# One decoder layer on one core: weight quantising cut into five pieces on GpSimd, down weights turned one stage earlier, the last tile in halves, the first batch in pairs with two gates made ahead

## What is computed

```
x = x + L0_attn(layernorm(x))          # products, running sums over tokens, products
x = x + L0_xattn(layernorm(x), ctx)    # causal softmax attention over the batch and 77 context rows, and a gate
x = x + L0_ffn(layernorm(x))
def fp4_quant_dequant(x):              # blocks of 16 along the last dim
    scale = max(max|x| / 6, 1e-12)     # then each value goes to the nearest of 0, .5, 1, 1.5, 2, 3, 4, 6 times scale
L0_ffn: gate, y = q(x) @ q(w_gate).T, q(x) @ q(w_up).T ; h = silu(gate) * y ; q(h) @ q(w_down).T
```

## Time and profile before

| | us |
|---|---|
| median of 3 runs (563.71 to 565.39) | 565.12 |
| the profiled execution's own time | 565.76 |
| its span, first to last instruction | 564.0 |
| PE busy in the span | 534.6 |
| DVE, ACT, POOL busy | 451.4, 341.1, 368.4 |

### The profile page before, as it was taken

One profiled execution on the slowest core, in us unless ns is written; L12 is line 12 of the kernel. 1 busy time (PEld: TensorE's weight loads), 2 busy tenths in 40 slices (PEclk: granted clock), 3 DMA queues, 4 the chain that ended last, 5 costly groups with the idle time before them and its releaser, 6 DMA issues.

```text
span 564.0 us, 10898 instructions
## 1 busy us (share of the span) xinstructions
PE 534.6 (95%) x3126; PEld 472.0 (84%) x3126; DVE 451.4 (80%) x1134; ACT 341.1 (60%) x802; POOL 368.4 (65%) x528
## 2 busy tenths in 40 slices
PE   4997999999999999999999998999999999999995
PEld 3876888888888888888888886899899999999985
DVE  3687679775798856886679948999899999999985
ACT  3435653736546256553395456888777887888752
POOL 4024927648358186384595925888988888888850
PEclk9998999999999999999999989899999999999999
DMA  7720400000000000000000000000000000000001
GB/s 213 200 90 5 151 2 0 2 2 0 0 0 0 0 0 2 1 2 1 0 2 1 1 1 1 2 19 19 19 19 19 19 19 19 19 27 19 20 20 47
DMA packets 16125, 13.79 MB, mean 24 GB/s; under 512 B 3883, under 2 KB 15839, under 8 KB 16095
## 3 DMA queue, kind: packets, MB, share of 16 engines
q1 hardware_dynamic: 16095, 13.43, 7.7%
HBM read 9.23 MB, written 4.19 MB: 24 GB/s over the span
## 4 chain that ended last, share of the span: by engine, by line
PE 76%; DVE 6%; ACT 4%; issue 4%; POOL 2%; ACTq 0%; DVEq 0%; POOLq 0%
PE ps L950 16%; PE ps L951 16%; PE ps L952 16%; PE ps L1150 10%; PE ps L1309 3%; PE ps L1138 3%; PE ps L1068 2%; PE ps L1069 2%; PE ps L1148 2%; PE ps L1040 1%; PE ps L1198 1%; ACT xn_sums L658 1%; PE ps L1077 1%; DVE X L1484 1%; PE ps L1325 1%
## 5 line engine op out<-in xcount | busy, mean ns | idle before, releaser
L950 PE MATMUL ps<-keys_h,nT_h 128*128 128x256 f32 (+6 forms) x272 | 86.0, 316 | 2.2 <-DVE keys_l L1390 1.5
L951 PE MATMUL ps<-keys_l,nT_h 128*128 128x256 f32 (+6 forms) x272 | 83.7, 308 | 0.0
L952 PE MATMUL ps<-keys_h,nT_l 128*128 128x256 f32 (+6 forms) x272 | 83.1, 306 | 0.0
L950 PE MATMUL ps<-parts,xq_parts 128*128 128x512 f32 (+1 forms) x192 | 76.0, 396 | 0.0
L951 PE MATMUL ps<-parts,xq_parts 128*128 128x512 f32 (+1 forms) x192 | 72.7, 379 | 0.0
L952 PE MATMUL ps<-parts,xq_parts 128*128 128x512 f32 (+1 forms) x192 | 72.4, 377 | 0.0
L1150 PE MATMUL ps<-V,probT 128*128 128x256 f32 x288 | 67.4, 379 | 0.0
L701 ACT ACTIVATE prob<-ps,nbias 128x205 f32<-128x205 f32 (+7 forms) x32 | 25.7, 804 | 67.2 <-DVE nbias L1470 67.2
L1150 PEld LDWEIGHTS ps<-V,probT 128*128 128x128 f32 x288 | 54.5, 189 | 7.7
L950 PEld LDWEIGHTS ps<-keys_h,nT_h 128*128 128x128 f32 x272 | 51.5, 189 | 6.2 <-issue 2.1
L951 PEld LDWEIGHTS ps<-keys_l,nT_h 128*128 128x128 f32 x272 | 51.5, 189 | 3.2
(11 more groups left out here) (227 smaller groups left out, 1607.5 us busy)
## 6 DMA issues: line engine op xcount, KB each, us to landing
X<-in_x_dram SPq DMA_DIRECT2D x8, 512.0 KB, 4.9
out_dram<-X SPq DMA_DIRECT2D x32, 128.0 KB, 1.7
early<-in_L_ffn_w_down_dram SPq DMA_DIRECT2D x1, 704.0 KB, 6.5
early<-in_L_ffn_w_gate_dram SPq DMA_DIRECT2D x1, 640.0 KB, 4.4
early<-in_L_ffn_w_up_dram SPq DMA_DIRECT2D x1, 640.0 KB, 4.8
ctx_rows<-in_ctx_dram SPq DMA_DIRECT2D x1, 308.0 KB
early<-in_L_attn_Winv_dram SPq DMA_DIRECT2D x1, 256.0 KB, 3.9
early<-in_L_attn_WQ_dram SPq DMA_DIRECT2D x1, 256.0 KB, 5.1
```

Of the source, the lines that this page charges most:

```text
L950: mm(o, wh, mh, start=start, stop=False, **kw)
L951: mm(o, wh, ml, start=False, stop=False, **kw)
L952: return mm(o, wl, mh, start=False, stop=stop, **kw)
```

## The change

The edits, each with the engines whose order they change:

- GpSimd's four passes over a quarter of the weights are each cut into five instructions of 224 columns.
- `turn_wd(0)` and `turn_wd(1)`, with ACT's copies and DVE's low parts, go from feed-forward steps 0 and 1 to the end of the last batch; part 2 goes behind `h_magnitude` on ACT and behind `h_rescaled` on DVE.
- The last tile (31) is quantised and turned in two halves of 384 and 320 columns; its first rounding half stands on DVE, its second on GpSimd; its three `gate_up` chunks are issued a step earlier.
- `xn` and `nrm` are signalled by pairs of tiles, so that PE can start turning after two of four.
- The gates of tiles 0 and 1 of each batch are made before the batch begins; `KEYS_BANK` changes to suit.
- PE has products whose result nothing reads (`keep_warm`): 12 before `make_inner`, 7 after it, 5 in step 0 of batch 0. PE's loop over the first two batches is written out.

```diff
-    KEYS_BANK = (1, 6)
-    GATES = [[0, 1], [2, 3], [], [], [4, 5], [], [6, 7], [], [], []]
+    KEYS_BANK = ((1, 3), (6, 7))
+    GATES = [[], [2, 3], [], [], [4, 5], [], [6, 7], [], [], []]
...
             def raw_scaled(b):
-                part, blk = raw_part(b)
                 wait_apart(0, s_raw_scales, b + 1)
-                g.tensor_tensor(blk, blk, wsc[:, 3, :].unsqueeze(2).broadcast_to([P, RBLK, QBLOCK]),
-                                ALU.mult).then_inc(s_raw_scaled, 1)
+                raw_by_blocks(b, 3).then_inc(s_raw_scaled, 1)
...
             def raw_rounded(b):
-                part, blk = raw_part(b)
                 wait_apart(1, s_raw_rounder, b + 1)
-                g.tensor_tensor(part, part, wm[:], ALU.add).then_inc(s_raw_sums, 1)
+                raw_with_rounder(b, ALU.add).then_inc(s_raw_sums, 1)
...
@@ scalar: xn_half, norm2_half
-                last.then_inc(s_xn, 1)
+                    if i % 2:
+                        last.then_inc(s_xn, 1)
...
@@ scalar, end of a batch
+                        if i == TPB + 1:
+                            gate_tile(b + 1, 0)
+                            gate_tile(b + 1, 1)
...
                         if i == TPB:
+                            wd_copy(0)
+                            wd_copy(1)
                             silu(0, 0, first=True)
...
@@ scalar, feed-forward step
-                if done == 1:
-                    wd_copy(0)
-                    wd_copy(1)
-                    wd_copy(2)
...
                 h_magnitude(n, first=(done == 0))
+                if done == 1:
+                    wd_copy(2)
+                if left == 1:
+                    silu(n + 1, 2)
...
@@ tensor
     def keys_products(b, h):
                 pe.wait_ge(s_nT_l, b * 4 + (h * 2 + 2))
+                if h == 0:
+                    pe.wait_ge(s_probT, START + b * CPB)
...
                         gate_up(0, 0, 0, first=True)
                         turn_tile(b, TPB - 1, (2,))
+                        turn_wd(0)
+                        turn_wd(1)
...
                         turn_nrm(b, 3)
+                        if isinstance(b, int) and b == 0:
+                            keep_warm(FIRST_WARM, 5)
...
                             keys_products(b + 1, 0)
+                            gate_tile(b + 1, 0)
+                            gate_tile(b + 1, 1)
...
+            def keep_warm(count, bank=1):
+
+                for _ in range(count):
+                    mm(ps[:, bank, :].rearrange("p (a n) -> p a n", n=P), ident16[:], ident16[:].unsqueeze(1).broadcast_to([P, 4, P]),
+                       start=True, stop=True)
+
+            pe.wait_ge(s_ident16, 1)
+            keep_warm(WARM_UP[0])
             make_inner()
+            keep_warm(WARM_UP[1])
...
-            with pe.Fori(0, B - 2) as b:
+            for b in range(B - 2):
                 batch(b, True, ahead=True)
...
                 if left >= 1:
                     gate_up(n + 1, 1 - u, 0)
+                if left == 1:
+                    gate_up(n + 1, 1 - u, 1)
+                    gate_up(n + 1, 1 - u, 2)
```

More of the change, by code:

```diff
@@ new lines, in raw_by_blocks, with raw_with_rounder @@
+            def raw_by_blocks(b, row):
+                for blocks, _, part in raw_pieces(b):
+                    blk = part.rearrange("p (b k) -> p b k", k=QBLOCK)
+                    last = g.tensor_tensor(blk, blk, wsc[:, row, blocks].unsqueeze(2).broadcast_to(
+                        [P, RBLK // RAW_PIECES, QBLOCK]), ALU.mult)
+                return last
+            def raw_with_rounder(b, op):
+                for _, cols, part in raw_pieces(b):
+                    last = g.tensor_tensor(part, part, wm[:, cols], op)
+                return last
@@ L834, in _ @@
             a.activation(proj_h[:, :, 5 * R:6 * R], xt[:], ACT.Copy)
+            act.wait_ge(prep_mm, 2)
+            for m in range(KD):
+                a.activation(pairs_of(proj_h[:, m, 0:4 * R]), bilinear_sums(m), ACT.Copy)
+                last = a.activation(pairs_of(proj_h[:, m, 3 * R:7 * R])[:, :, R:2 * R], trilinear_sums(m), ACT.Copy)
+            last.then_inc(prep_ev, 1)
             act.wait_ge(s_rstd1, 2)
@@ L1349, in _ @@
                 step(pr * 2 + 5, 1)
-            for n in range(NT - 4, NT):
-                step(n, n % 2, left=NT - 1 - n)
-            h_turn(NT - 2)
-            down(NT - 3, 1)
-            h_turn(NT - 1)
-            down(NT - 2, 0)
-            pe.wait_ge(s_hh, NCH * NT)
-            down(NT - 1, 1, bank=0)
+            for n in range(NT - 4, LAST):
+                step(n, n % 2, left=LAST - n)
+            h_turn(LAST - 2)
+            down(LAST - 3, 0)
+            h_turn(LAST - 1)
+            down(LAST - 2, 1)
+            for k in range(2):
+                if k == 0:
+                    pe.wait_ge(s_hq, LAST + 1)
+                else:
+                    pe.wait_ge(s_hq_twice, LAST + 1)
+                for t in range(3):
+                    last = turn(ps[:, k, t * P:(t + 1) * P], end_hq[:, (k * 3 + t) * P:(k * 3 + t + 1) * P], ident[:])
+                last.then_inc(s_hq_turned, 1)
+            down(LAST - 1, 0)
+            pe.wait_ge(s_hqT_l, LAST + 2)
+            down(LAST, 1, bank=2)
         @block.vector
@@ L1633, in step @@
                     x_scaled(n + 3, 1 - u)
-                if done == 1:
-                    wd_low(0)
                 h_max(n)
@@ L1648, in step @@
                     h_rescaled(n - 1, 1 - u, first=(done == 1))
+                if done == 1:
+                    wd_low(2)
             def batch(b, more, ahead=False):
```

193 lines of the change are left out of this document (141 added, 52 removed).

## The result

| | before | changed |
|---|---|---|
| median of four runs each, us | 565.21 | 557.88 (556.84 to 560.95) |
| ratio, with its 95% interval | | 0.9885 [0.984, 0.9931] |
| the profiled execution, us | 565.76 | 556.84 |
| its span, us | 564.0 | 554.9 |

The change made the kernel faster by 7.3 us, 1.2%. The prediction was 554.3 with a range of 550.5 to 558.5. The median lies in the range near its upper end; the ratio applied to the 565.1 of before gives 558.6, just outside. A second set of six runs of the changed kernel gave 558.32 (556.99 to 559.69), ratio 0.9874 [0.9845, 0.9902]. So the sign was right, and of the forecast gain of 10.8 us 3.5 are missing in the first set (10.8 - 7.3) and 4.0 in the second, where the kernel before took 565.11.

What follows compares the result with a forecast made beforehand. PE, busy 534.6 of 564.0 us, was taken to bound the kernel. Terms of 2.0 + 2.7 + 0 + 3.4 + 0.3 + 2.4 = 10.8 us bring the profiled 565.76 to 555.0, as a median 554.3, range 550.5 to 558.5.

Steps and rivals of the forecast that it cites:

- Start: Kernel start: added products give PE full rate, `xn` pairs let turning begin sooner; 2.0 us gained, bounds 1.0 and 2.4.
- First batch: Batch 0, logits 0 to key products: gates ahead, pairs and added products take 7.5 instead of 10.24; 2.7 us gained.
- GpSimd itself: GpSimd's passes in pieces: 2.8 us more a batch, covered by its 12.79 us of idle time before L446.
- a new PE hole: Sign in the profile after: a new PE hole in the loop would make the prediction wrong; no size given.
- Later batch starts: Three later batch boundaries: one wait of about 0.3 us exchanged for another; 0 in sum, each between -0.4 and +0.4.
- Last batch: Last batch: GpSimd's pieces free DVE, removing PE's hole and the low clock behind it; 3.4 us gained, bounds 1.5 and 4.3.
- feed-forward start: Start of feed-forward: moved copies bring `round_x(4)` earlier but `h_turn(0)` is late next; 0.3 us gained, bounds -0.5 and +1.1.
- End: Kernel end: last tile's halves ready earlier, PE's holes shrink from 2.67 + 1.47 to 1.8; 2.4 us gained, bounds 1.2 and 3.0.
- Low clock stays: Rival, 13 in 100: added products do not bring PE to full rate at the start and in batch 0; 559.0 us.
- Pieces do not free DVE: Rival, 12 in 100: GpSimd's next piece wins over the waiting DVE instruction, the last batch gives nothing; 557.7 us.
- New waits at the seams: Rival, 10 in 100: each batch start loses 0.4 and the feed-forward start 0.5 by new waits; 556.3 us.
- GpSimd becomes the chain: Rival, 3 in 100: dearer pieces, 11.2 us in four batches, hold up `mix_tile(6)` through `base_tiles(6, 7)`; 568.9 us, slower.

Runs made afterwards that it cites:

- experiment 2: Changed kernel with GpSimd's `base_tiles` of tiles 0 and 1 ahead of the second half of the values: 554.33 us, ratio 0.9815.
- Experiment 8: Experiment 2's kernel with the gates of tiles 0 and 1 back in step 0 of their own batch: 554.04 us, ratio 0.9801.
- experiment 7: Kernel before the change with only GpSimd's four passes cut into five instructions each: 561.13 us, ratio 0.9922.
- experiment 9: Experiment 2's kernel with `wd_copy(2)` ahead of `h_magnitude(1)` on ACT in feed-forward step 1: 551.78 us, ratio 0.9759.
- 6: Changed kernel with GpSimd's four passes whole again, one instruction of 1120 columns each: 561.95 us, ratio 0.9948.
- the repeat: Changed kernel run again unaltered, six runs: 558.32 us, ratio 0.9874.
- experiments 4: Changed kernel without any of the 24 added PE products: 559.1 us, ratio 0.9895.
- 5: Experiment 2's kernel without any of the added PE products: 557.4 us, ratio 0.9842.
- 11: Experiment 9's kernel without the five added products in step 0 of batch 0: 552.24 us, ratio 0.9762.
- experiments 10: Experiment 9's kernel with gates ahead in batch 0 alone, ACT's and DVE's loops over the first two batches written out: 551.03 us, ratio 0.9737.
- 12: Experiment 9's kernel with GpSimd's passes in two instructions of 560 columns instead of five: 552.36 us, ratio 0.9766.

## Why the prediction was right and wrong

**Start (2.0, measured 2.7).** Right in mechanism: the durations, not the printed clock, told the rate. The window over the first 14 us printed 1.00 before and the same products took 2.08 then and 1.16 us now. The excess of 0.7 over the term, and of 0.3 over its upper bound, is at least partly scatter from one execution to another: with the added products the first projection started at 15.98 to 17.36 in ten traces, without them at 17.97 to 18.68. That scatter is wide enough that one pair of traces does not size the term. The prediction prices a slow start twice, at 2 us lost here and at 1 in the rival; no run had it. That the printed 1.00 was the absence of a record is a reading that no run tests; the durations alone are shown.

**First batch (2.7, measured 2.8 to the key products and 0.4 to the end of the batch).** This is the step that failed. The working ended at the key products and handed its gain on to the end of the batch, with the next wait for GpSimd put at nothing. "GpSimd itself ... 2.8 us a batch, covered by idle time" priced GpSimd only for its pieces, in a later batch, where it stood idle for 12.79 us. In batch 0 its chain left PE 1.6 us, and moving PE by 5.4 made it the limit. That it was a new PE hole which could make the prediction wrong was written down; where it would open was not looked for, although DVE's first `mix_tile` at 67.3 was at hand. The hole took 2.76 us (experiment 2), and 1.4 more by the clock in one of the two profiled executions of the changed kernel.

**Later batch starts (0, measured 0.07 and -0.24).** Right as a sum. Experiment 8 splits it: gates ahead cost 0.5 to 0.6 us a batch, and by subtraction the pairs and pieces give about as much back.

**Last batch and feed-forward start (3.4 + 0.3, measured 3.5).** Right as a sum, with both terms mis-sized. The pieces alone give 4.4 (experiment 7), of which 2.7 are holes and the rest the low clock. Gates ahead took 0.4 of it, and what is left for the moved down weights, put at +0.3, is 139.34 - 0.44 - 138.45 = 0.45 us slower, near its lower bound. That is a difference of three executions: no run has the down weights' move alone. The wait that was named for it ("DVE waits in `wd_low(2)`") is real, and experiment 9 removed it for 2.4 us. That `h_turn` would stay late was seen, but not that ACT had 1.09 us idle just ahead.

**End (2.4, measured 2.8).** Right; the one hole is 1.30 where 1.8 was forecast.

**The rivals.** *Low clock stays* did not happen where it was placed: no window from 48 to 62 us is low in either execution of the changed kernel. *Pieces do not free DVE* is refuted by 6 and 7. *New waits at the seams* was right in kind: 0.24 in batch 2 and 0.45 at the feed-forward start. *GpSimd becomes the chain* came nearest: it names `base_tiles` holding up `mix_tile`, which is the wait that opened. But it puts it at tiles 6 and 7 of every batch, for the dearer pieces, with no gain on DVE; it opened at tile 0 of batch 0, for the order of the values, ahead of every piece there, and cost 2.8 and not 11.2.

**The missing part.** In the profiled executions the gain is 8.9 us (565.76 to 556.84), so 1.9 of the 10.8 are missing: the hole took 2.76, and all other terms together gave 0.9 more than forecast. The medians miss 3.5. The other 1.6 come from which executions were profiled: that of the changed kernel is the fastest of its four, 1.0 under their median, and that of the kernel before stands 0.55 over its own. The 1.0 fits a clock that falls behind the hole in some runs (1.37 in the repeat); it was seen in the one that was profiled, and for the others only their mean clock speaks.

## What to carry to other kernels

When an edit moves the limiting engine forward in one place, follow that engine to the next thing that it takes from each other engine, and write down how long that one had been ready. An engine that is "covered by idle time" is so in a stage, not in a kernel: GpSimd had 12.79 us idle in one batch and left PE 1.6 in another. And where one engine's long instruction holds up another engine, try it in pieces. Here the DVE instructions beside a whole pass of 2.6 us ended with it. Two pieces gave back 2.2 of the 2.7 us that this cost PE, five the rest, and a pass in five took GpSimd 3.5 us.

## What was not expected of the hardware

A hole does not always bring the clock down. Behind the same wait (2.55 and 2.56 us) it stayed at 1.00 in one execution and read 0.57 over the next 4 us in another, and behind one of 1.45 us it fell in experiments 4 and 5 and not in 11. The two sets of the changed kernel spread over 4.1 and 2.7 us, and experiment 9, without the hole in batch 0 and the wait of 1.70 us, over 0.17. Not all spread is the clock's: experiments 10 to 12 spread over 1.2 to 1.5 us with a mean clock of 0.997 or more. And a fall can be free: at the feed-forward start the stage took 139.3 us with and without one, since PE's later waits shrank by what it lost; that ACT and DVE set the pace there is how I read it. The bill is to be made from stage lengths, not from the windows that read 0.50.
